# One graph layer on one core: the attention values are normalised and weighed one step later on VectorE

## The reference

```python
w_phys = (silu(rbf @ w1 + b1) @ w2 + b2) * cutoff[:, None]
msg_phys = xn[col] * w_phys
q_e, k_e, v_e = (Q[row], K[col], V[col])
scores = jnp.sum(q_e * k_e, axis=-1) / np.sqrt(HD) * cutoff[:, None]
attn = jax.nn.softmax(scores, axis=1)            # over the 8 heads of one edge
msg_attn = (attn[..., None] * v_e).reshape(-1, H)
aggr = segment_sum(msg_phys + gate * msg_attn, row, num_segments=n)
return x + aggr @ wo + bo
```

## Time and profile before

| | before |
|---|---|
| runs | 5468.53 us (5467.22 to 5485.16) |
| profiled execution | 5472.01 us, its span 5470.3 us |
| PE, PEld busy | 5173.4 us (95%), 3821.0 us (70%) |
| DVE busy | 4191.7 us (77%) |
| ACT busy | 3927.3 us (72%) |
| POOL busy | 3975.5 us (73%) |
| DMA | 1306.16 MB, mean 239 GB/s; 333 to 339 GB/s in the edge stage |
| L1031 POOL gathers | 1760, 1228 ns each |
| L1217 DVE query_key | 880, 688 ns each |
| L1222, L1229, L1255 DVE | 440 each, 1216, 1220 and 1225 ns |

### The profile page before, as it was taken

How to read it: one execution, slowest core, us unless ns; L and a number is a source line. 1 busy time by engine, 2 the same in 40 slices (tenths; PEclk the granted TensorE clock), 3 DMA queues, 4 the chain that set the end, 5 groups by cost and what they waited for, 6 DMA issues and landing times. The chain is left out here.

```text
span 5470.3 us, 117155 instructions
## 1 busy us (share of the span) xinstructions
PE 5173.4 (95%) x24352; PEld 3821.0 (70%) x24353; DVE 4191.7 (77%) x7424; ACT 3927.3 (72%) x12601; POOL 3975.5 (73%) x3476
## 2 busy tenths in 40 slices
PE   3779999999999999997799999999999999999999
PEld 3556666666666666675577777777777777777777
DVE  9789986666655655322788888888888888888894
ACT  4546666666666666665688888888888888888883
POOL 1567777777777777767578888888887888888880
PEclk9989999999999999998899999999999999999999
DMA  6233444444434444443999999999999999999956
GB/s 199 93 106 128 148 164 161 133 161 159 161 130 167 157 153 143 162 144 135 339 333 336 332 337 336 333 333 335 334 337 335 336 336 333 334 337 335 338 187 190
DMA packets 584400, 1306.16 MB, mean 239 GB/s; under 512 B 81246, under 2 KB 384134, under 8 KB 582961
## 3 DMA queue, kind: packets, MB, share of 16 engines
q0 software_dynamic: 221536, 881.08, 44.4%
q1 hardware_dynamic: 311796, 345.48, 21.1%
q10 hardware_dynamic: 50850, 77.03, 3.9%
HBM read 1024.15 MB, written 324.38 MB: 247 GB/s over the span
## 5 line engine op out<-in xcount | busy, mean ns | idle before, releaser
L1031 POOL DMA_INDIRECT ukvx<-kvx_table,urec x1760 | 2161.6, 1228 | 589.5 <-issue 532.0
L341 POOL DMA_INDIRECT records<-rows,slot_i x1660 | 1746.7, 1052 | 679.2 <-issue 470.1
L696 PE MATMUL w_ps<-w2s,hid 128*128 128x256 f32 x6656 | 1551.0, 387 | 51.7 <-DVE rows L610 51.5
L696 PEld LDWEIGHTS w_ps<-w2s,hid 128*128 128x128 f32 x6656 | 1247.7, 192 | 374.7 <-issue 156.2
L610 DVE TENSOR_TENSOR rows<-w_ps,b2b 128x512 f32<-128x512 f32 x832 | 571.5, 687 | 742.5 <-PE w_ps L696 742.2
L810 ACT ACTIVATE hid<-hid_ps,b1t 128x512 f32<-128x512 f32 x832 | 526.2, 683 | 817.6 <-PE hid_ps L685 802.8
L1153 PE MATMUL ag_ps<-ukvx,uonehot 128*128 128x256 f32 x3520 | 982.0, 402 | 0.2 <-issue 0.2
L1133 PE MATMUL uq_ps<-aggr,uonehotT 128*128 x3520 | 972.9, 399 | 2.1 <-ACT uonehotT L1048 1.0
L1158 PE MATMUL ag_ps<-ukvx,uonehot 128*128 128x256 f32 x3520 | 935.1, 388 | 24.6 <-issue 24.5
L1158 PEld LDWEIGHTS ag_ps<-ukvx,uonehot 128*128 128x128 f32 x3520 | 642.3, 190 | 191.6 <-issue 116.8
L1075 ACT ACTIVATE uexp<-uscores,umax 128x8 f32<-128x8 f32 x1760 | 507.4, 289 | 368.8 <-DVE umax L1239 365.7
(11 more groups left out here) (175 smaller groups left out, 5065.4 us busy)
## 6 DMA issues: line engine op xcount, KB each, us to landing
urec<-records SPq DMA_DIRECT2D x880, 260.0 KB, 6.1
rbf_in<-in_edge_attr SPq DMA_DIRECT2D x207, 256.0 KB, 3.0
kvx_table<-kvx ACTq DMA_DIRECT2D x10, 3456.0 KB, 14.5
ukvx<-kvx_table,urec POOLq DMA_INDIRECT x1760
records<-rows,slot_i POOLq DMA_INDIRECT x1661, 2.5
records<-kvx SPq DMA_DIRECT2D x1, 13000.0 KB
aggr<-query_table SPq DMA_DIRECT2D x7, 1792.0 KB, 19.2
fbase<-x_plus_h SPq DMA_DIRECT2D x14, 896.0 KB, 7.0
```

What stands on the lines that cost most here:

```text
L341: pool.indirect_dma_start(recs, bass.IndirectOffsetOnAxis(ap=slot_i[:, q, t:t + 1], axis=0), rows[:, q, t, :], None).then_inc(scattered[q] ...
L696: m = pe.matmul(w_ps[j % 2][:, h, :], hid[:, k % 2, c, h, j * P:(j + 1) * P], w2s[:, c, :], start=(h == 0 and c == 0), stop=(c == 1), skip ...
L1031: pool.indirect_dma_start(kvx[:, k, j, :], None, table, bass.IndirectOffsetOnAxis(ap=rec[:, k, j, R_DST:R_DST + 1].bitcast(I32), axis=0), ...
```

## The change

In VectorE's even step, normalise and attend of the pair behind are taken out; in its odd step they stand behind query_key and ahead of score, two units behind, which from an odd unit is the same pair. Invert stays in the even step. The three calls that close the last pair stay too; the constant `U` is only written out.

```diff
                 if k % 2 == 0:
                     physical(u, k, i, first)
                     behind(invert, 1, u, k, i, first)
-                    behind(normalise, 1, u, k, i, first)
-                    behind(attend, 1, u, k, i, first)
                 else:
+                    behind(normalise, 2, u, k, i, first)
+                    behind(attend, 2, u, k, i, first)
                     score(u, k, i, first)
                     weigh(u, k, i, first)
                     maximum(u, k, i, first)
             turns(dve, unit)
-            U = UNITS
-            before = (U - 1, DEPTH - 1, TURNS - 1, False)
+            before = (UNITS - 1, DEPTH - 1, TURNS - 1, False)
```

## The result

| | before | after |
|---|---|---|
| median of four runs each, taken side by side | 5472.3 us | 5591.15 us (5582.2 to 5599.98) |
| ratio | | 1.0214 (1.0195 to 1.0233) |
| profiled execution, its span | 5472.01, 5470.3 us | 5582.2, 5580.5 us |

What follows compares the result with a forecast made beforehand. VectorE's own sequence was taken as the bound (6.03 us a pair); under the change held gathers make pairs 6.39, a turn 31.95 against 30.78, +103 us on 5472, 5575, median 5571. Range 5395 to 5720.

Steps and rivals of the forecast that it cites:

- The free pair (step 1): VectorE's time for two units if nothing else is late: 5.76 us, a gain of .27 on 6.03 from shorter drain gaps.
- TensorE and the ring (step 2): Later av_done costs nothing (1.3 us left); the chain through ring maximum and exponents needs 5.63 us a pair, below 5.76.
- GpSimd (step 3): Fourth gather, due at 5.92, falls .16 us behind physical at 5.76 and is held; three gathers start where four are needed.
- one resting pair: Edge stage settles from any start into pairs of 2.09 + D, 6.39 us, physical waiting for the gather physical held.
- D: Time from a gather's end to its data's landing, taken as 4.3 us; the forecast case, D 4.0 to 4.7, had 0.61.
- the 5575 of my sum: Forecast of the profiled execution: 5472 plus 103 us; the median was put 3.5 us lower, at 5571.
- The gathers fit after all: Rival on GpSimd: all four gathers fit into VectorE's pair of 5.76 us, turn 29.43, time 5350 us; chance 0.14.
- Waits and gain cancel: Rival: edge-stage turns of ten units come out between 30.6 and 31.0 us; chance 0.07.
- landing late in full: Rival: gathered data land late, D of 4.7 and more, pairs of 6.8 and more, time above 5720 us; chance 0.04.
- The 5.93 window: Rival: D below 3.84, pairs of 5.93 just let the fourth gather in before physical, time 5410 us; chance 0.12.
- the rival that put the time at 5710: A gather also holds VectorE's weigh for .95 us in each pair; chance 0.02.

Runs made afterwards that it cites:

- one_gather: Changed kernel with the second half's gather of each unit left out, so half the gathered rows are never loaded: 5301.75 us, ratio .9683 to before.
- three pad runs: Changed kernel with a useless VectorE sum over 96, 256 or 512 constants ahead of the even query_key: 5596.75, 5381.64 and 5494.9 us.
- pad256: Changed kernel with a useless VectorE sum over 256 constants ahead of the even query_key: 5381.64 us, ratio .9837 to before.
- later_pad384: Changed kernel with attend moved behind score and a useless 384-number VectorE sum ahead of the even query_key: 5343.11 us, ratio .9755 to before.
- the other order: Changed kernel with attend moved behind score: 5500.04 us; with a useless 256-number VectorE sum added, 5344.3 us.

## Why the prediction was right

1. **The free pair (step 1).** Predicted 5.76, measured 5.63: query_key to normalise .57 for .61, invert to query_key .09 for .17 (my lower bound was .10), physical .60 for .61, attend to score 1.14 as said. The gain is .40 a pair and not .27. The .17 does appear in one_gather (4000.85 to 4001.02), where TensorE is the bound. This miss mattered little, since the pair is not the pace.

2. **TensorE and the ring (step 2)** were no bound: 31.7 + 7.6 us of waits for attend in the whole stage, 68 and 22 times (the second being PE's own row beside PEld's). The 5.74 that I read from the earlier trace rows proved to be the floor when the gathers were taken away.

3. **GpSimd (step 3).** Held gathers end 2.10 behind attend and physical, as said; the fourth starts at 5.81 where I had 5.92 (attend starts at 2.09 and not 2.21); it falls .18 behind physical where I had .16. Both ends of the comparison moved together, by .11 and .13, as nearly all of what I had too long lies ahead of attend, and so in both. What decides is therefore the stretch from attend to the next physical: 3.54 here, where the fourth gather comes 3.71 behind attend. The three pad runs put the step where this says, above 5.71 and not above 5.87.

4. **The price.** Here the reasoning was right in kind and wrong in its picture. I had one resting pair, 2.09 + D with D = 4.3, 6.39, and held that any start runs into it. Counted over all pairs of the trace but the first few, the mean is 6.46, but four gathers start in 311 of them, three in 66 and five in 57. 170 needed a gather that a physical had held: mean pair 6.75, median D 4.64. In 266 the gather had passed, mostly ahead of physical as at 4015.49: mean pair 6.27, median D 5.76. A long pair lets the next gather in front of physical, which makes the next pair short, and then the gather falls behind again. D was undersized by .34 where the formula held, and the formula held in four pairs of ten only; the two errors offset each other. In the traced execution the stage, from its first physical to its last, grew by 117 us (2727.5 to 2844.8) where I had 103, and the rest of the program came out 7 shorter, so that this execution, at 5582, is 7 above the 5575 of my sum. The other 13 of the 20 us are the spread between executions: I took the median as 3.5 below the traced one, and it lies 9 above it. So the size came out right in part by luck: with the true D of 4.64 and the one picture, pairs of 6.73 would have given the top of my range. The rows that I took D from were narrower than I said, too: the landings of 4.3 to 7.2 us, median 6.5, are those of 4000 to 4100 us; over 2720 to 5330 us the same view gives 2.7/6.1/7.2, so a D below 3.84 was not under all that was seen.

5. **The rivals.** "The gathers fit after all" lost by .18 us: pad256 is its world, with added work. "Waits and gain cancel" and "landing late in full" lie on either side of the mean turn that came, 5 x 6.46 = 32.3: it is above 31.0, and below the 34 of pairs of 6.8. The 5.93 window did not come, as D is over 3.84 in most pairs. The rule of the Trainium skill, SBUF — State Buffer, section "Who interferes with whom", that the shared port is an exclusive lock and the order of issue decides who blocks (that the first keeps it for its whole instruction is written there of VectorE's 2-port modes, and I carried it over to two inputs), failed in the same direction as before: physical at 4011.20 starts under a gather .06 us old and takes 1.22. By the rule that physical would have been held to 4012.15, the gather's end, and the pair of pad256 would be some .95 us longer, an estimate; it was 5.87. Weigh was held by none either: in the changed kernel 393 weighs between 2650 and 5200 us start inside a gather and take .19 or .20 us, so the rival that put the time at 5710 had no such hold. This shows that a gather does not hold VectorE for its 1.01 us; whether it uses the port for a moment at its start only, no run tells.

## What to carry to other kernels

When two engines block each other in one direction only, compare start times over one period and not busy shares: here the fourth gather was .18 us late, and moving it cost .24 us a pair and gave 210 us. An order that makes the leading engine faster can bring its blocking instruction in front of a step that used to slip past, so look at what stands just ahead of and just behind it, at both ends of the gap; and if a trace shows that, lengthen the stretch between the two blocking instructions (here attend to the next physical) a little before giving up the order; a delay that stands ahead of both moves everything alike. Where the starving is intermittent, estimate the mean from both kinds of period, the held and the passed.

## What was not expected of the hardware

- The hold is decided at the gather's start. A gather of 1.01 us that started .06 us (pad256) or .19 us (later_pad384) ahead of physical was not lengthened, although physical ran over nearly all of it; one that started .18 behind took 1.92. Over the 13 traces the edge is sharp, and it lies just behind VectorE's start: all 33 gathers that started up to .02 us behind a physical or an attend kept 1.0 us, of the 22 at .03 and .04 seven were held, and all 8721 from .05 to 1.07 ended 2.08 to 2.13 us behind that start. That is 1.09 and the usual 1.01, as if a held gather began anew 1.09 us behind that start.
- More work on VectorE made the program faster by 210 us (5591 to 5382), and by 156 us in the other order (5500 to 5344), while the same work in the old order cost 87.
- An instruction behind a reciprocal that it does not read starts .09 us after it, below the .10 that I had taken as the least.
- The time from a gather's end to its use in pairs that waited had a median of 5.3 us (319 pairs up to 5440 us; nine of ten between 4.2 and 6.6), with a DMA share of .92 in the stretch shown above.
